# Page loop of a two-layer transformer kernel: last keys' values by SyncE's copies onto a zeroed diagonal, not by masks on GpSimd

## The reference, cut to what matters

```python
k_blocks = k_blocks.at[blk, :, off, :].set(k.transpose(0, 2, 1, 3))   # the new tokens' keys and values
v_blocks = v_blocks.at[blk, :, off, :].set(v.transpose(0, 2, 1, 3))   # go into the pages
...
scores = jnp.einsum('bghtd,bgsd->bghts', qg, k_all) * SCALE
allowed = (kpos[None, None, :] <= pos[:, :, None]) & (kpos[None, None, :] > pos[:, :, None] - WINDOW)
p = jax.nn.softmax(jnp.where(allowed[:, None, None, :, :], scores, -jnp.inf), axis=-1)
o = jnp.einsum('bghts,bgsd->bghtd', p, v_all)
```

## Time and profile before

| | us |
|---|---|
| median of three timed runs | 584.53 (583.47 to 586.75) |
| the profiled execution, own time | 580.49 |
| its span, first to last instruction | 578.70 |
| mean granted TensorE clock | 0.931 of full speed |

### The profile page before, as it was taken

The page is one execution under the profiler, slowest core; times in us unless marked ns, Lnnn a source line. Parts: engine busy times, 40 slices in busy tenths (PEclk is TensorE's granted clock), DMA queues, the critical chain, the costliest instruction groups (busy, mean ns, idle before and its releaser), DMA issues. The chain is left out here.

```text
span 578.7 us, 10881 instructions
## 1 busy us (share of the span) xinstructions
PE 495.7 (86%) x4207; PEld 375.7 (65%) x4207; DVE 359.3 (62%) x777; ACT 252.8 (44%) x548; POOL 261.9 (45%) x240
## 2 busy tenths in 40 slices
PE   2997799999998999998879899477999998199956
PEld 0686368886886788776644347356777775099846
DVE  2757478886686878845676555953466886334412
ACT  6287753343432444243872334363355544034420
POOL 5055435463443677775650000378572017445640
PEclk9799999999999999999999899756699999689987
DMA  5564681000000121230000009511000002498326
GB/s 172 185 253 171 263 242 42 1 1 1 0 1 1 37 71 57 68 102 16 2 3 1 1 1 353 192 40 26 14 26 5 3 1 82 158 332 257 112 71 195
DMA packets 24723, 51.53 MB, mean 89 GB/s; under 512 B 4264, under 2 KB 16705, under 8 KB 23520
## 3 DMA queue, kind: packets, MB, share of 16 engines
q1 hardware_dynamic: 18704, 40.62, 20.4%
q0 software_dynamic: 5968, 10.22, 5.9%
HBM read 43.99 MB, written 12.37 MB: 97 GB/s over the span
## 5 line engine op out<-in xcount | busy, mean ns | idle before, releaser
L753 PE MATMUL ps<-x_split,gate_up_split 128*128 128x512 f32 x384 | 96.3, 393 | 0.1
L753 PEld LDWEIGHTS ps<-x_split,gate_up_split 128*128 128x128 f32 x384 | 72.0, 188 | 17.1 <-issue 1.5
L2055 POOL DMA_INDIRECT wbig<-new_kv,prepi x40 | 42.4, 1059 | 79.8 <-DVE wmid L1443 68.7
L940 POOL TENSOR_TENSOR gate_up_split<-wbig,gate_up_split 128x768 fp32r<-128x768 f32 (+1 forms) x24 | 41.5, 1731 | 52.3 <-ACT gate_up_split L882 52.2
L864 DVE TENSOR_TENSOR hidden_split<-work,hidden_split 128x512 fp32r<-128x512 f32 x34 | 37.7, 1109 | 23.1 <-ACT hidden_split L929 23.1
L775 PE MATMUL ps<-hidden_split,down_split 128*128 128x512 f32 x160 | 42.5, 395 | 2.6 <-issue 1.4
L1995 POOL DMA_INDIRECT chosen<-work,wbig x31 | 30.5, 984 | 30.8 <-ACT work L1980 16.6
L929 ACT ACTIVATE hidden_split<-work 128x512 fp32r<-128x512 f32 x34 | 21.4, 630 | 50.6 <-DVE work L859 48.4
L946 POOL TENSOR_TENSOR down_split<-wbig,down_split 128x384 fp32r<-128x384 f32 (+1 forms) x24 | 29.1, 1213 | 25.9 <-ACT down_split L889 25.8
L2055 POOL DMA_INDIRECT wbig<-in_cache_dram,prepi x32 | 33.5, 1047 | 7.6 <-issue 6.9
L775 PEld LDWEIGHTS ps<-hidden_split,down_split 128*128 128x128 f32 x160 | 29.8, 188 | 10.7 <-issue 4.2
(11 more groups left out here) (337 smaller groups left out, 1180.1 us busy)
## 6 DMA issues: line engine op xcount, KB each, us to landing
work<-in_wE_dram SPq DMA_DIRECT2D x1, 5376.0 KB, 16.1
wbig<-in_wF_dram SPq DMA_DIRECT2D x3, 1664.0 KB, 7.0
sorted<-wmid SPq DMA_DIRECT2D x1, 3999.0 KB, 16.8
wbig<-in_wG_dram SPq DMA_DIRECT2D x1, 3072.0 KB, 10.3
wbig<-in_wE_dram SPq DMA_DIRECT2D x6, 384.0 KB
wbig<-chosen SPq DMA_DIRECT2D x8, 256.0 KB, 5.1
wbig<-sorted SPq DMA_DIRECT2D x1, 1935.0 KB, 12.8
wmid<-in_wE_dram SPq DMA_DIRECT2D x5, 384.0 KB
```

The lines of the kernel that those rows point to most:

```text
L753: mm = nc.tensor.matmul(o, self.gus[:, w % 2, a, 2 * m + k, :], self.xs[:, b, k, n * HALF:(n + 1) * HALF], start=(k == 0 and a == b), stop ...
L940: nc.gpsimd.tensor_tensor(self.gus[:, k % 2, 1, 0:self.gu_chunks], self.gate_up[:, :, j * P:(j + 1) * P], self.gus[:, k % 2, 0, 0:self.gu_ ...
L2055: return nc.gpsimd.indirect_dma_start(dst, None, table, bass.IndirectOffsetOnAxis(ap=rows.bitcast(U32), axis=0), **({} if bound is None el ...
```

## The change

Three things change. (1) `vlast` is zeroed once, both halves, by GpSimd; then only the four blocks on the diagonal are written, per group by four copies of 32 rows x 128 values within SBUF, issued by SyncE. Their semaphores are page_vlast0 and page_vlast1. The zeros stay, since later groups write the same blocks. (2) In SyncE's stream the two writes of new_kv come first, then the 32 copies with their waits, then w_high and w_low. (3) `wo_turned` moves within wmid, to make room for the early zeroing.

```diff
-        wo_turned = cut(wmid, 2048, 512).rearrange("p (c k) -> p c k", c=KC)
+        wo_turned = cut(wmid, 1280, 512).rearrange("p (c k) -> p c k", c=KC)
...
             def values(q4):
                 pe.wait_ge(sem("page_lT"), q4 + 1)
                 pe.wait_ge(sem("page_pT"), 4 * q4 + 4)
-                pe.wait_ge(sem("page_vlast"), q4 + 1)
+                pe.wait_ge(sem(f"page_vlast{q4 % 2}"), 16 * 4 * (q4 // 2 + 1))
...
             sp.wait_ge(sem("lin_scaled"), 16)
             sp.wait_ge(sem("lin_mem"), 4)
-            by_expert = wE_d.rearrange("(e p) f -> p e f", p=P)
-            sp.dma_start(w_high, by_expert[:, LOW:NE + 1, :]).then_inc(sem("ld_wE"), 16)
-            sp.dma_start(w_low, by_expert[:, 0:LOW, :]).then_inc(sem("ld_wE_low"), 16)
             for n in range(2):
                 sp.wait_ge(sem("page_rot"), n + 1)
                 sp.wait_ge(sem("page_v_raw"), n + 1)
                 sp.dma_start(new_kv[n * HALF:(n + 1) * HALF, :].rearrange("(g p) f -> p g f", p=P),
                              newkv[:, 4 * n:4 * n + 4, :]).then_inc(sem("page_new"), 16)
+            for q4 in range(B // 4):
+                sp.wait_ge(sem(f"overlay{q4 % 4}"), 16 * 5 * (q4 // 4 + 1))
+                if q4 == 0:
+                    sp.wait_ge(sem("page_token"), 2)
+                if q4 >= 2:
+                    sp.wait_ge(sem("page_pv"), q4 - 1)
+                for j in range(4):
+                    own = slice(32 * j, 32 * j + 32)
+                    sp.dma_start(vlast[own, q4 % 2, j, :], kv[own, B + q4, P:2 * P]).then_inc(sem(f"page_vlast{q4 % 2}"), 16)
+            by_expert = wE_d.rearrange("(e p) f -> p e f", p=P)
+            sp.dma_start(w_high, by_expert[:, LOW:NE + 1, :]).then_inc(sem("ld_wE"), 16)
+            sp.dma_start(w_low, by_expert[:, 0:LOW, :]).then_inc(sem("ld_wE_low"), 16)
...
             order = [t for q4 in range(B // 4) for t in [B + q4] + list(range(4 * q4, 4 * q4 + 4))]
+            pool.wait_ge(sem("page_ms"), 4)
+            nc.gpsimd.memset(vlast.rearrange("p r b f -> p (r b f)"), 0.0).then_inc(sem("page_token"), 1)
             pool.wait_ge(sem("page_new"), 32)
-
-            def last_values(q4):
-                pool.wait_ge(sem(f"overlay{q4 % 4}"), 16 * 5 * (q4 // 4 + 1))
-                if q4 == 0:
-                    pool.wait_ge(sem("fold_done"), 1)
-                if q4 >= 2:
-                    pool.wait_ge(sem("page_pv"), q4 - 1)
-                nc.gpsimd.tensor_tensor(vlast[:, q4 % 2], kv[:, B + q4, P:2 * P].unsqueeze(1).to_broadcast([P, 4, P]),
-                                        const("quad").unsqueeze(2).to_broadcast([P, 4, P]), ALU.mult)\
-                    .then_inc(sem("page_vlast"), 1)
-
             pool.wait_ge(sem("page_rot"), 2)
             for n, t in enumerate(order):
                 q4 = n // 5
                 if q4 >= 4 and n % 5 == 0:
                     pool.wait_ge(sem(f"overlay{q4 % 4}"), 16 * 5)
                 gather(kv[:, t, :], new_kv, new_rowi[:, t:t + 1], T - 1).then_inc(sem(f"overlay{q4 % 4}"), 16)
-                if n % 5 == 4 and n >= 10:
-                    last_values(n // 5 - 2)
-            last_values(B // 4 - 2)
-            last_values(B // 4 - 1)
             moe.gpsimd(pool)
```

## The result

The changed kernel takes 598.14 us, the median of four runs (596.83 to 603.13), where the kernel before took 584.66 us in the four beside it (583.47 to 586.75). The ratio is 1.024 with a 95% interval of 1.019 to 1.029. That is 15 us more than forecast, beyond the range, and on the side of the slower cases. The profiled execution took 596.83 us, its span is 595.0 us against 578.7 us, and the mean granted clock 0.920 against 0.931.

A forecast was written before the change was run, and what follows sets the result against it. TensorE, busy for 86% of the span, was taken to bound the kernel, with gathers beside it costing some 1.6 us a group. Two groups' -3.25 and one's +1.6 gave -1.65 us: 584.53 to 582.9 us, range 578.0 to 590.3 us.

The forecast's parts named there:

- Masks off GpSimd: GpSimd in the page loop: 8.3 us of mask work and 22.3 us of waiting go; directly 0, off the path.
- Zeroing: GpSimd ahead of the gathers: the added zeroing of 128x1024 takes 0.88 us, hidden in idle time, so 0.
- New keys first: SyncE's queue: new_kv's write lands 2.8 us earlier, first gather starts at 367.0 us; 0 on the path.
- Gathers without stops: GpSimd in the page loop: gathers end at 420.7 us, freeing two groups of losses of 1.66 and 1.59 us.
- Copies: SyncE in the page loop: 32 added copies, issued in 0.47 us each, covered by 3 us or more: 0.
- Experts' weights: Load moved behind the last copies: upper part ready at 470.9 us, lower by 473.7; 0, with 4.2 us cover.
- Sum: Whole kernel: two groups lose 3.25 us, one may gain up to 1.6; total -1.65 us, ends -3.25 and 0.
- A: Page loop: the loss goes with each gather wherever it lies, net 0, 584.5 us; chance 0.20.
- B: TensorE's clock in the page loop: full clock returns one group later, +9.0 less 3.25, 590.3 us; chance 0.22.
- C: TensorE's clock in the page loop: full clock returns a group earlier, up to -9.0 us, 575.5 us; chance 0.15.
- D: Experts' weights land too late beside dense TensorE code and routing: +1 to +3 us more, 586.5 us; chance 0.07.
- if TensorE waits for a copy: Page loop: TensorE waiting for a copy before its value matmuls would show the whole account wrong; no size given.

The follow-up runs named there:

- e2: The changed kernel without its 32 copies, the last keys' values left zero: 598.5 us, ratio 1.028 to the kernel before.
- e3: The changed kernel with GpSimd's old waits for TensorE's values put back from the twenty-fifth gather on, without the masks: 590.67 us, ratio 1.011 to the kernel before.
- e4: The changed kernel with a GpSimd product of 128x512 on a spare buffer after each five gathers from the fifteenth on: 590.22 us, ratio 1.005 to the kernel before.
- e8: The changed kernel with both the 128x512 spare products after each five gathers and the masks' old waits: 583.44 us, ratio 0.998 to the kernel before.
- e9: The changed kernel with a small GpSimd product of 128x8 after every second gather from the fourteenth on: 581.48 us, ratio 0.988 to the kernel before.
- e1: The changed kernel with the experts' weights asked for ahead of the writes of new_kv again: 604.25 us, ratio 1.031 to the kernel before.

## Why the prediction was wrong

**Masks off GpSimd: directly 0.** Right: TensorE never waited for a mask before, nor for a copy now.

**Zeroing, 0.88 us, hidden.** Right: 0.95 us, followed by 4.22 us of idling.

**New keys first, gathers from 367.0 us.** Right: 367.70 us.

**Gathers without stops, until 420.7 us.** The timing is nearly right: the last ends at 422.5 us, forecast was 420.7 us. The last groups are free of gathers and the four that begin at full clock take 7.5 us each, as forecast for two of them (7.6 us). The five together gain 10.3 us, more than the 3.25 us counted, because the low clock's group is no longer among them.

**Copies: 0.** Right. Issuing one took 0.51 to 1.6 us, in the median 0.59, not 0.47, and e2 without them is no faster.

**Experts' weights: 0, with 4.2 us of cover.** Right: they landed in 17.7 us instead of 16.1, and 4.9 us were left.

**Sum.** This is the step that failed. It let one group "gain the same loss, from 0 to +1.6" and took +1.6 us. Measured are holds of 4.1, 7.3, 3.7, 8.0 and 0.9 us in the chain, 23.9 us in all, and a loss of 25.0 us up to the third group's keys, of which the groups behind give 10.3 us back. (The sum's own upper end of 0 comes from none of its terms either; they give -3.25 to -1.65.) The rows for the 1.6 us were true, but they came from a kernel in which GpSimd stopped after each fifth gather from the fifteenth on. e3, e4 and e8 give such stops back and the loss goes, in e8 all of it. So the size was read from rows of the very condition that the change removed. The term *Masks off GpSimd* names the removed stop ("Indirectly GpSimd no longer stops between gathers"), and *Gathers without stops* then uses it only to shorten the gathers. The correlation of gathers with a delayed TensorE was seen and called a correlation. That late updates queue up behind each other, so that the price grows along a row of gathers, was not in it. What it lacked was a bound from above, which no row gave: the longest row of gathers in a row before was fifteen, and that fifteenth ends at 391 us, just where the first hold begins.

**A** (the loss goes with each gather wherever it lies) named the right operations but gave them a fixed price. The loss is not fixed per gather. Forty gathers cost 24 us in a row, and in pairs, as in e9, some 3 us. The Trainium skill (SBUF — State Buffer, "Who interferes with whom") says of the ports of SBUF that a DMA never contends with a compute engine and that TensorE and ScalarE never wait on anyone. For the ports these runs say nothing against it, since TensorE's single matmuls are no longer than before (L1485: 273 ns in the median in both traces). But who waits for TensorE's results got them up to 20.1 us late, and by that rule alone the change would have cost nothing.

**B** (the full clock comes back one group later, 590.3 us) was on the right side, and its trigger, TensorE held after the clock had risen, is what happened: the clock was 0.97 at 392 to 395 us, 0.50 from 395 us on, and came back only at 432 us. Its price was the clock's alone, +9.0 us, and the holds' own length was not in it. **C** and **D** did not occur; e1, with the weights ahead, rules D out as a part of the cause.

The sign that the prediction named for failure, "if TensorE waits for a copy", did not come up. The one that did was in the same paragraph under A: more gaps of the kind of the earlier trace rows before 421 us. They were there with ten times the length.

## What to carry to other kernels

A removed operation removes its wait too, and a wait can be what others live on: before taking work from an engine that issues a long row of indirect DMAs, ask what happened in its pauses. Read the price of an effect only from rows in which the condition is as it will be after the change; if there are none, bound it by the whole stretch, not by the largest instance seen. On a GpSimd with dozens of gathers beside dense TensorE work, try a tiny operation and its wait after each second gather; it is a change of a few lines. That it helps is measured in this kernel alone.

## What the runs showed that was not expected

- While GpSimd issues gathers of 128 rows x 256 values every 1.30 us, from about the sixteenth on, the updates of TensorE's semaphores come late, in their order, and ever later: 4.2 us at first, 20.0 us at the worst. TensorE's own instructions run at their usual length, and the profile can't name the releaser.
- Stops of GpSimd let them through. With a short stop of about 1 us after each gather no wait of this kind exceeded 0.6 us on TensorE; after each second or third they reached 3.2 us, after each fifth 4.9 us, without stops 11.2 us (14.6 us in e1).
- The stop may be an operation on unrelated data or plain waiting; a longer one (1.05 us of work instead of 0.2) came with about 1% less time, though it also lowers the rate of the gathers.
- A product of 128x8 on GpSimd takes 0.21 us, but with the wait for its own end the next gather starts 0.77 us after it.
- Holds and the clock go together: in the page loop, 1.2 GHz was last granted until 417 us before, until 432 us after, and until 410 us with twenty gathers.
